# Layer 2's output tiles in a row, its roots and transposition earlier, the first norm's result written in step 3

## What is computed

```
x  = _layernorm(x + _L0_attn_ref(x, ...))          # layer 1's product, then the first norm
     # Q, K, V = _multilora(x, ids, W, A, B); Q, K = _rope(Q), _rope(K)
     # attn = softmax(causal(Q K^T / sqrt(32))); out = _multilora(attn V, ids, Wo, Ao, Bo)
x  = _layernorm(x + _L0_ffn_ref(x, ...))
     # attn = _attention(_rmsnorm(x, ln1_w), Wq, Wk, Wv, Wo); mod = 0.1 * tanh(attn @ A)
     # h = _rmsnorm(x, ln2_w); gate = silu(h @ W_in_base.T + mod * (h @ A) @ B)
     # residual + (gate * (h @ W_up_base.T)) @ W_down.T
```

## Time and profile before

| | before |
|---|---|
| time, median of 3 runs | 2786.15 us (2785.99 to 2786.51) |
| the profiled execution's own time | 2788.6 us |
| its span | 2786.8 us |
| PE busy | 2629.9 us, 94% |
| DVE, ACT, POOL busy | 1600.0 us (57%), 1325.7 us (48%), 667.9 us (24%) |
| granted clock of PE, mean | 0.98 |

### The profile page before, as it was taken

The page is one execution under the profiler, slowest core; times in us unless marked ns, Lnnn a source line. Parts: engine busy times, 40 slices in busy tenths (PEclk is TensorE's granted clock), DMA queues, the critical chain, the costliest instruction groups (busy, mean ns, idle before and its releaser), DMA issues.

```text
span 2786.8 us, 40960 instructions
## 1 busy us (share of the span) xinstructions
PE 2629.9 (94%) x13584; PEld 2019.6 (72%) x13584; DVE 1600.0 (57%) x4341; ACT 1325.7 (48%) x2739; POOL 667.9 (24%) x535
## 2 busy tenths in 40 slices
PE   6999999999888999999999889999999999999998
PEld 5777777777566666666666647888888888888886
DVE  5777777777847788787787774222222423333333
ACT  3777777777734666666666674111111321111111
POOL 4556555556321322222222221000000000000000
PEclk9999999999889999999999979999999999999999
DMA  6565556665545664565554534111111311111100
GB/s 148 113 146 138 138 124 142 147 144 130 148 120 125 133 131 106 132 132 102 127 132 103 125 83 161 47 47 47 47 47 47 115 47 47 47 47 47 47 30 30
DMA packets 174634, 276.44 MB, mean 99 GB/s; under 512 B 29556, under 2 KB 53876, under 8 KB 173940
## 3 DMA queue, kind: packets, MB, share of 16 engines
q1 hardware_dynamic: 170884, 259.98, 39.1%
q0 software_dynamic: 2304, 12.58, 1.3%
q10 hardware_dynamic: 1264, 1.64, 0.2%
HBM read 97.03 MB, written 42.99 MB: 50 GB/s over the span
## 4 chain that ended last, share of the span: by engine, by line
PE 54%; DVE 9%; issue 3%; ACT 2%; DMA 2%; SPq 1%; POOL 0%; ACTq 0%; DVEq 0%; POOLq 0%
PE lin_ps L2575 13%; PE b_scores_ps L2586 13%; PE b_pv_ps L2556 6%; PE b_scores_t_ps L2556 6%; PE lin_ps L2104 5%; PE b_pv_ps L311 2%; DVE b_prob L294 2%; DVE b_junk L206 2%; PE b_scores_t_ps L275 2%; PE lin_ps L2067 2%; PE b_scores_ps L192 1%; DMA b_k_stack<-b_k_split 1%; PE lin_ps L2581 1%; PE b_scores_ps L2049 1%; SPq L262 1%
## 5 line engine op out<-in xcount | busy, mean ns | idle before, releaser
L286 ACT ACTIVATE b_prob<-b_scores_t_ps 128x384 fp32r<-128x384 f32 (+1 forms) x384 | 201.1, 524 | 218.1 <-PE b_scores_t_ps L277 198.9
L294 DVE TENSOR_TENSOR a_prob<-a_scores_t_ps,a_prob 128x384 fp32r<-128x384 f32 (+1 forms) x384 | 225.3, 593 | 135.7 <-ACT a_scores_t_ps L287 134.2
L294 DVE TENSOR_TENSOR b_prob<-b_scores_t_ps,b_prob 128x384 fp32r<-128x384 f32 (+1 forms) x384 | 225.8, 592 | 100.1 <-ACT b_scores_t_ps L287 100.0
L286 ACT ACTIVATE a_prob<-a_scores_t_ps 128x384 fp32r<-128x384 f32 (+1 forms) x384 | 201.7, 525 | 156.4 <-PE a_scores_t_ps L277 130.8
L311 PE MATMUL b_pv_ps<-b_prob,b_value 128*33 128x512 f32 (+3 forms) x1024 | 273.6, 336 | 0.1
L311 PE MATMUL a_pv_ps<-a_prob,a_value 128*65 128x512 f32 (+3 forms) x1024 | 271.1, 333 | 0.4 <-DVE a_prob L294 0.2
L206 DVE CUSTOM_DVE_ANT_0 b_junk<-b_scores_ps,spare 128x512 bf16<-128x512 f32 (+3 forms) x512 | 226.8, 483 | 66.3 <-PE b_scores_ps L192 63.8
L206 DVE CUSTOM_DVE_ANT_0 a_junk<-a_scores_ps,spare 128x512 bf16<-128x512 f32 (+3 forms) x512 | 226.6, 483 | 26.9 <-PE a_scores_ps L192 24.8
L2519 DVE TENSOR_TENSOR res<-b_scores_ps,b_first_gate 128x512 f32<-128x512 f32 x64 | 44.3, 692 | 331.9 <-PE b_scores_ps L2586 331.9
L2519 DVE TENSOR_TENSOR stage<-b_scores_ps,b_junk 128x512 f32<-128x512 f32 x64 | 44.3, 692 | 328.2 <-PE b_scores_ps L2586 328.2
L1143 PE MATMUL lin_ps<-x_split,w_split 128*128 128x512 f32 x768 | 216.7, 397 | 1.5 <-DVE w_split L938 1.2
(11 more groups left out here) (318 smaller groups left out, 5908.8 us busy)
## 6 DMA issues: line engine op xcount, KB each, us to landing
a_q_stack<-a_q_split SPq DMA_DIRECT2D x192, 128.0 KB, 3.4
a_k_stack<-a_k_split SPq DMA_DIRECT2D x192, 128.0 KB, 3.5
b_q_stack<-b_q_split SPq DMA_DIRECT2D x192, 128.0 KB, 3.1
b_k_stack<-b_k_split SPq DMA_DIRECT2D x192, 128.0 KB, 3.7
spare<-h_t SPq DMA_DIRECT2D x16, 1024.0 KB, 6.2
stage<-in_x_t SPq DMA_DIRECT2D x8, 1024.0 KB, 6.5
a_sum_hi<-a_pv_raw SPq DMA_DIRECT2D x32, 256.0 KB, 3.8
a_inverse_all<-softmax_sums SPq DMA_DIRECT2D x32, 256.0 KB, 3.5
```

The lines of the kernel that those rows point to most:

```text
L286: act.activation(at.prob_hi[:, k % at.ring, 0:w], at.scores_t_ps[:, k % 2, 0:w], ACT.Exp, scale=SCALE)
L294: dve.tensor_tensor(at.prob_lo[:, k % at.ring, 0:w], at.scores_t_ps[:, k % 2, 0:w], at.prob_hi[:, k % at.ring, 0:w], ALU.subtract).then_in ...
```

## The change

In layer 2, for each of the seven passes that have a next one:

- The four output tiles are made in a row, from step 0's unit 7 to step 1's unit 2, 6 or 7 matmuls a unit. The q and k of step 3 move two units back to make room (step 1's units 3 to 6), `h_times_a` two units ahead (units 8, 9).
- Residual adds and statistics are taken apart and spread over step 0's unit 9 to step 1's unit 8. The two roots are found side by side: the second starts from the variance directly, so a reciprocal, a product, a sum's wait and the product at the end are gone. Roots are made in step 1's units 8 and 9, h rows in 9 and 10 (before 10 and 11).
- POOL's h tiles stand at the end of its step 1 (before at the head of step 2), the transposition in step 1's unit 11 and step 2's units 0 to 2 (before units 1 to 4), the next pass's q and k of step 0 in step 2's units 4 to 6 (before 6 to 8).
- x1 is written in step 3's units 4, 7, 8, 8 (before step 2's units 8 to 11), and stored one place later on SP.

In layer 1's prologue the remainders of Wv go from POOL to DVE, ahead of the rotations, ACT's Wv copies stand ahead of the first projected tiles, and the six small DMAs (`send_b(0)`, `send_low(0)`) go from ACT's queue to SP's, behind all loads of weights.

The core of the diff (layer 2):

```diff
-MADE_B = (((-2, 6, 8, -2, 8), (-2, 6, 9, -2, 9)), ((-3, 10, 12, -2, 3), (-2, 0, 2, -2, 4)),
-          ((-2, 3, 5, -2, 5), (-2, 5, 7, -2, 7)), ((-2, 1, 3, -2, 3), (-2, 3, 5, -2, 5)))
-OUT_SLOTS = (7, 5)
-OUT_COUNT = (6, 4)
-H_LO = 2
+MADE_B = (((-2, 4, 6, -2, 6), (-2, 5, 7, -2, 7)), ((-3, 10, 12, -2, 3), (-2, 0, 2, -2, 4)),
+          ((-2, 3, 5, -2, 5), (-2, 5, 7, -2, 7)), ((-2, 3, 5, -2, 5), (-2, 5, 7, -2, 7)))
+OUT_SLOTS = (7, -1)
+OUT_COUNT = (4, 4)
+TURN_SLOTS = (11, 12, 13, 14)
+X1_SLOTS = (4, 7, 8, 8)
...
-                dve.wait_ge(ln_step, done + TT + 1)
-                dve.reciprocal(newton[:, 0, :], squares[:, 0, :]).then_inc(ln_step, 1)
-                dve.wait_ge(ln_step, done + TT + 2)
-                dve.tensor_tensor(newton[:, 1, :], newton[:, 0, :], mean_var[:, :, 1], ALU.mult).then_inc(ln_step, 1)
-                dve.wait_ge(ln_step, done + TT + 3)
-                dve.tensor_scalar(squares[:, 1, :], newton[:, 1, :], RMS_EPS, None, ALU.add).then_inc(ln_step, 1)
+                dve.tensor_scalar(squares[:, 1, :], mean_var[:, :, 1], 1.0 + RMS_EPS, LN_EPS * RMS_EPS, ALU.mult,
+                                  ALU.add).then_inc(ln_step, 1)
...
-            def both_roots(b):
-                dve.wait_ge(ln_step, b * LN_STEPS + TT + 4 + RSQRT_STEPS)
-                dve.tensor_tensor(inv_root[:, 1, :], inv_root[:, 0, :], inv_root[:, 1, :], ALU.mult).then_inc(ln_step, 1)
...
-                    if g == 1 and slot == 10 and not last:
-                        variances(b + 1)
...
+                    if g == 0 and slot == 10 and not last:
+                        statistics(b + 1, 0)
+                    if g == 1 and slot in (0, 2, 8) and not last:
+                        statistics(b + 1, 1 + (0, 2, 8).index(slot))
...
-                    if g == 0 and slot == 10 and not last:
-                        add_residual(b + 1, 0)
+                    if g == 0 and slot in (9, 11) and not last:
+                        add_residual(b + 1, (9, 11).index(slot))
                     if g == 1 and not last:
-                        if slot in (1, 7, 9):
-                            add_residual(b + 1, 1 + (1, 7, 9).index(slot))
-                        if slot == 10:
+                        if slot in (1, 3):
+                            add_residual(b + 1, 2 + (1, 3).index(slot))
+                        if slot == 8:
+                            variances(b + 1)
                             root_start(b + 1)
                             root_round(b + 1, 0)
-                        if slot == 11:
+                        if slot == 9:
                             for i in range(1, 3):
                                 root_round(b + 1, i)
-                            both_roots(b + 1)
-                            h_rows(b + 1, 0)
-                            h_rows(b + 1, 1)
+                        if slot in (9, 10):
+                            h_rows(b + 1, slot - 9)
...
-                    if g == 2 and not last:
-                        if slot >= UNITS - TT:
-                            normalise_tile(b + 1, slot - (UNITS - TT))
-                        if H_LO <= slot < H_LO + TT:
-                            h_tile(b + 1, slot - H_LO)
+                    for t in turned(b, g, slot - 1):
+                        h_tile(b + 1, t)
...
+                    if g == 3 and not last:
+                        for x in range(TT):
+                            if X1_SLOTS[x] == slot:
+                                normalise_tile(b + 1, x)
...
-                    if g == 1 and slot in (10, 11):
-                        h_times_a(b, share(3 * KC, 2, slot - 10))
-                    if g == 2 and 1 <= slot < 5 and not last:
-                        turn_h(b + 1, slot - 1)
+                    if g == 1 and slot in (8, 9):
+                        h_times_a(b, share(3 * KC, 2, slot - 8))
+                    for t in turned(b, g, slot):
+                        turn_h(b + 1, t)
```

More of the change, by code:

```diff
@@ L755, in step @@
                         rope(*tile)
-            pool.wait_ge(w_ready, 2 * KC)
-            for c in range(KC):
-                pool.wait_ge(w_hi, 2 * KC + c + 1)
-                pool.tensor_tensor(w_split[2][:, 1, c, :], w_stage[2][c], w_split[2][:, 0, c, :],
-                                   ALU.subtract).then_inc(w_ready, 1)
-            pool.wait_ge(const_in, 80)
             for i in range(2):
@@ L878, in _ @@
             adapter(0)
[L879 to L883 removed]
             weights(0)
             low(0)
[L886 to L890 removed]
+            for n in range(1, 3):
+                weights(n)
             for i in range(2):
                 projected(0, 0, i)
[L893 removed]
             for i in range(2):
@@ L1065, in _ @@
             constants()
+            weights(2)
             for i in range(2):
@@ L1285, in out_items, with turned @@
             yield from range(n * half + share(half, OUT_COUNT[n], at).start, n * half + share(half, OUT_COUNT[n], at).stop)
+def turned(b, g, slot):
+    for t in range(TT):
+        if (g - 1) * UNITS + slot == TURN_SLOTS[t] and not is_last(b):
+            yield t
 def gate_value_items(b, g, slot):
@@ L1424, in gate_layer @@
         z_out = sem("z_out")
[L1426 removed]
+        LN_STEPS = TT + 2 + RSQRT_STEPS
         qk_ready = (at.q_ready, at.k_ready)
@@ L1517, in step @@
                     gather(*group(b, g, -1))
-                if g == 3 and not last:
-                    store_x1(b + 1)
                 if g == 2 and not last:
@@ L1633, in body @@
                 for g in range(GROUPS):
-                    if g == 2 and has(b, 1):
-                        for t in range(2, TT):
-                            normalise_tile(b + 1, t)
                     if is_last(b) and g == 0:
@@ L1654, in body @@
                         weigh(*group(b, g, -1))
+                    if g == 1 and has(b, 1):
+                        for t in range(2, TT):
+                            normalise_tile(b + 1, t)
             batches(pool, body, 2)
@@ L1773, in step @@
                             z_part(b - 1)
-                    if g == 2 and slot == 0:
+                    if g == 1 and slot == 10:
                         h_times_a(b)
@@ L1785, in step @@
                         mlp.input_hi(act, mlp.start, slot - 5)
-                    if g == 2 and 2 <= slot < 6 and not last:
-                        h_tile(b + 1, slot - 2)
+                    for t in turned(b, g, slot - 1):
+                        h_tile(b + 1, t)
                     for to in left_b(b, g, slot):
@@ L1846, in add_residual, with statistics @@
                 dve.tensor_tensor(res[:, t, :], lin_ps[:, t % 2, :], res[:, t, :], ALU.add).then_inc(o_added, 1)
+            def statistics(b, t):
                 dve.wait_ge(o_added, b * TT + t + 1)
@@ L1988, in step @@
                             projected(*to)
+                    if g == 3 and not last:
+                        for x in range(TT):
+                            if X1_SLOTS[x] == slot:
+                                normalise_tile(b + 1, x)
             for t in range(TT):
                 add_residual(0, t)
+                statistics(0, t)
             variances(0)
@@ L2058, in project_out @@
                     bank = t % 2
-                    if y == 0 and not (isinstance(b, int) and b == 0):
-                        pe.wait_ge(qk_ready[bank], b * GROUPS - 1 + t // 2)
-                    elif y == 0 and t >= 2:
+                    if y == 0 and t >= 2:
                         pe.wait_ge(o_added, b * TT + t - 1)
+                    elif y == 0 and not (isinstance(b, int) and b == 0):
+                        pe.wait_ge(qk_ready[bank], b * GROUPS - 1)
                     if y < 3 * KC and b == 0 and t < 2:
@@ L2079, in turn_h @@
                     pe.wait_ge(h_hi, b * TT + t - 1)
+                elif isinstance(b, int) and b == 0:
+                    pe.wait_ge(o_added, 3 + t)
                 else:
-                    pe.wait_ge(o_added, b * TT + 3 + t)
+                    pe.wait_ge(qk_ready[bank], b * GROUPS)
                 for c in range(KC):
```

24 lines of the change are left out of this document (8 added, 16 removed).

## The result

The changed kernel takes 2811.17 us (median of 4 runs, 2809.35 to 2819.67) where the kernel before, timed with it, takes 2786.33. The ratio is 1.0096, with a 95% interval of 1.0083 to 1.0108. The forecast was 2796 with a range up to 2810: the direction was right, but the loss is about two and a half times the forecast one, and the time lies just outside the range.

What follows compares the result with a forecast made beforehand. PE bounds steps 0 and 1, DVE and ACT step 1's unit 8 through step 2, a late transfer step 3's head. -2.0 - 0.8 + 22.8 + 0 - 12.6 + 2.1 = +9.5 us; forecast 2796, range 2770 to 2810.

Steps and rivals of the forecast that it cites:

- Prologues: Layer 1's Wv work and rotations, -2.0 us; four dependent operations fewer in layer 2's prologue, -0.8 us.
- rule about rings: Layer 1's low-rank rows, sent from SP's ring, come last behind the weights: term +1 us instead of -2.
- PE load in PE-bound units: Step 0 and step 1's units 0 to 4 get 14 more matmuls, 3.26 us a pass; +22.8 us in seven passes.
- The stretch to step 3: Step 1's unit 5 to step 3: 14 matmuls fewer, but new waits replace them; 0 us, +-14.
- That list: Expected profile: steps of the same pass near 26.0, 29.2, 25.6 and 24.8 us.
- the rival: Clock falls behind new waits in units 10, 11 and the transposition, once a pass: +8.4 us, 2804; chance 0.14.
- q and k sooner: Next pass's stacking DMAs leave two units sooner: waits go, -10.2 us, and two half-clock windows, -2.4 us.
- x1 in step 3: Four DVE operations of 0.65 us move from step 2 ahead of step 3's remainders: +0.3 a pass, +2.1 us.
- Costed at nothing: Effects given 0 us: earlier first residual add, POOL's h tiles, h times A and its copy, x1's later store.
- x's landing: First residual add one unit sooner, while its x may be landing: 0 us; without cover 1 us a pass.
- rival 3: Step 3's k stack lands late, a DMA wait of 1 us a pass: +7 us, 2803; chance 0.08.

Runs made afterwards that it cites:

- e3: The kernel before with only the change's edits in layer 1's prologue; ratio 0.9992 to the kernel before, interval holds 1.
- e9: e5 with four more unread matmuls ahead of step 2's transposition, waiting only for the last row maximum; ratio 1.0008 to the kernel before.
- e1: The changed kernel with x1 written in step 3's units 8, 8, 9, 9 instead of 4, 7, 8, 8; ratio 1.0039 to the kernel before.
- e10: The kernel before with x1 alone moved, from step 2's units 8 to 11 to step 3's units 8, 8, 9, 9; 2.8 thousandths faster.
- e8: e1 with k of step 3 made in step 1's units 7 and 8 instead of 5 and 6; 17 us slower than e1.
- e4: The kernel before with step 3's q and k made two units later in the last pass alone; ratio 0.9990 to the kernel before, interval holds 1.
- e2: The changed kernel with h times A back in step 1's units 10 and 11, its copy in step 2's unit 0; 21 us slower than the change.
- e5: e1 with six unread matmuls added at the end of step 1's unit 9 in seven passes; 3.6 us faster than e1 by the ratios.

## Why the prediction was wrong, point by point

- **Prologues, -2.0 and -0.8.** About right: -3.1 in the trace until layer 2 starts, -2.2 by e3's ratio. The +1 that the prediction made of the Trainium skill's rule about rings is not borne out (2.0 to 3.5 us of wait for 2.9 to 3.8).
- **PE load in PE-bound units, +22.8.** Right. Step 0 grew from 23.41 to 25.64 us in pass 2, by 2.2 for the 2.56 forecast; step 1's first five units by 0.7, for 0.7. Over the seven passes it is 21.1 us.
- **The stretch to step 3, 0.** Here lies the first failed step: it measured +10.2 us (308.4 for 298.3 in seven passes). The chain itself held unit by unit: step 2's unit 2 began 20.0 us behind step 1's unit 5 in pass 2, forecast 16.5 + 3.7 = 20.2. In e9, which has no fall of the clock, the stretch takes 299.3 us, so 9.2 of the 10.2 are gone; steps 1 and 2 take 29.0 and 26.54 us in pass 5, for the 29.2 and 25.6 listed. (That list has step 2 at a gain of 0.8 which the sum had put at nothing; there was no such gain.) I computed the new waits rightly, counted them at their own length, and gave what follows from them a chance of 0.14. The reason I gave against it was that one wait of 1.53 us had left the clock up. But here the waits come in pairs: behind 1.05 and 1.46 the clock fell in three passes of seven, behind 1.1 to 1.6 and 0.67 in six of seven, and in step 3 behind 0.52 and 1.67 in three of three. That is 12 falls where the rival had seven, and two before. Their price can be read in the change itself: step 1 takes 29.6 us on average with a fall and 28.5 without, step 2 27.9 with and 26.5 without, so 1.1 and 1.4 us a fall.

  That it is the closeness of two waits that matters is inferred, not shown: the kernel before has 0.7 and 1.4 us 4.5 us apart in all seven passes and no fall behind them, the pairs here are 1.1 to 4.0 us apart, and the same 1.05 and 1.46 left the clock up four times. (The wait of 0.69 us that the forecast reads at unit 10 of step 1 stands at the head of unit 11.)
- **q and k sooner, -12.6.** The DMA waits went, as forecast. With x1 out of the way (e1) step 3 is 13.0 us shorter than before. But most of the gain was not tied to the two units: e10 has 9.9 of it by taking one 0.54 us operation from in front of the split.
- **x1 in step 3, +2.1.** The second failed step, wrong in kind. At unit 4 it meets POOL's subtractions in passes 1, 3 and 5, waits for them, and PE and the clock follow. With the term before, step 3 was to lose 10.5 us and lost 1.2; e1 gives 11.9 of it back. Moved to where DVE idles, x1 brings no wait of PE's there (0.7 us a pass of step 3 are idle in e1), and alone it is a gain (e10).
- **Costed at nothing:** x's landing. DVE does now wait for it at the first add, 2.3 us at most, six times, but PE's idle time in step 0 is unchanged: 0.7 us a pass. The stack of step 3's k came in time, so rival 3 did not occur; e8 shows that its slack was indeed small.
- **Not in the sum:** the last pass, -6.8 us in the trace. I had counted q and k of step 3 for seven passes and not looked at the eighth. It is in part the edits there, in part time at half clock that this one execution was spared (e4). It is luck for the forecast: without it the time would lie farther outside the range.

The sum for the first seven passes was 22.8 - 12.6 + 2.1 = +12.3 us. They grew by 30.1, which is 21.1 from PE's load, 10.2 in the stretch and -1.2 in step 3: the two failed steps miss by about the same, 10.2 and 9.3. Without the falls of the clock and without the collision (e9) the passes grew by 9.2, although ten matmuls a pass are added. Of the gap of 20.9 between the change and e9, moving x1 gave 8.5 (e1); the other 12.4 are what the fills gave back. By the ratio alone, e1 would stand at 2797, beside the forecast of 2796. That is no support for the rest of the sum, since e1 still has ten falls of the clock, and gains in the last pass that nobody forecast.

## What to carry to other kernels

Where a change leaves TensorE with new short waits close together, price them at more than their length (1.1 to 1.4 us a fall here): look for the granted clock behind each, and put work ahead of the wait, not behind it in the same unit, since the engine goes in order. Before a large reordering is made to let one transfer start sooner, look at what stands directly ahead of the instruction that it waits for: here one operation of half a microsecond was the whole wait in four passes of seven. And a DVE operation from SBUF to SBUF belongs where POOL rests.

## What the runs showed of the hardware

- Adding 16.3 us of matmuls that nobody reads made the kernel 9 us faster (e1 to e9), while in layer 2's first seven passes the granted clock stayed at 1.00 instead of falling 10 times to half. The Trainium skill ("TensorE: Matmul & The Clock Gate", on the gate) says that idleness brings the clock down and activity releases it; e2, e5 and e9 agree, in both directions.
- A DVE operation of 0.54 us (one SBUF tensor) took 2.50 us beside three POOL subtractions of 1.28, 1.27 and 1.45 us in a row, and 2.45 to 2.52 in five passes of e2. The Trainium skill ("SBUF — State Buffer", on the two sides) says that GpSimd shares a port pair with DVE's instructions in a two-port mode or with two SBUF inputs, that whoever starts first holds it for its whole instruction, and that the other blocks. The trace agrees with the blocking (no run here shows the mode), with something more: DVE ended 0.28 us behind the end of the second of POOL's instructions, so it got through only there and not behind the one that was running.
- The same code scattered: layer 2 began between 843.6 and 852.3 us in ten traces with the same layer 1. A difference of a few microseconds between two single traces says nothing here.
